# Linear attention with routed experts on one core: an earlier exponential table, a reordered key phase, and key features of five batches made by VectorE

## The reference, cut to what matters

```
xn   = layernorm(x)                        # per token, eps 1e-5
q, k = elu(xn @ Wq.T) + 1, elu(xn @ Wk.T) + 1     # 16 heads of 8
kv   = sum over the tokens of a batch of k^T v ; k_sum = sum of k
att  = (q kv) / (q k_sum + 1e-6) @ Wo.T
aff  = xn @ centroids.T ; e = argmax(aff) ; alpha = sigmoid(max aff)
h    = relu((layernorm(xn) * g[e] + b[e]) @ w1[e].T + b1[e])
out  = x + att + xn + alpha * (h @ w2[e].T + b2[e])
```

## Time and profile before

| | |
|---|---|
| median of 3 runs | 155.09 us |
| profiled execution | 155.4 us, span 153.6 us, granted clock 0.995 |
| PE busy | 138.0 us (90%) |
| DVE busy | 111.8 us (73%) |
| ACT busy | 101.4 us (66%) |
| POOL busy | 115.4 us (75%) |
| chain that ended last | PE 72%, POOL 9%, DVE 7%, ACT 5%, DMA 3% |

### The profile page before, as it was taken

The page is one execution under the profiler, slowest core; times in us unless marked ns, Lnnn a source line. Parts: engine busy times, 40 slices in busy tenths (PEclk is TensorE's granted clock), DMA queues, the critical chain, the costliest instruction groups (busy, mean ns, idle before and its releaser), DMA issues.

```text
span 153.6 us, 4729 instructions
## 1 busy us (share of the span) xinstructions
PE 138.0 (90%) x1138; PEld 131.5 (86%) x1138; DVE 111.8 (73%) x395; ACT 101.4 (66%) x334; POOL 115.4 (75%) x137
## 2 busy tenths in 40 slices
PE   3945999896999999999999999999999999999930
PEld 3945898796988998899999999999999999999920
DVE  3999998999968988897856554667777756556440
ACT  7533988999448786886666657666666666666610
POOL 7644430899958867888887768878888888877774
PEclk9999999999999999999999999999999999999997
DMA  4999200499937999677678998877777777841111
GB/s 142 327 323 420 94 4 0 151 344 294 274 89 214 241 340 286 163 201 192 161 195 233 287 338 205 216 190 207 196 166 174 189 160 174 135 41 53 51 51 51
DMA packets 26601, 29.10 MB, mean 189 GB/s; under 512 B 3024, under 2 KB 20432, under 8 KB 26448
## 3 DMA queue, kind: packets, MB, share of 16 engines
q1 hardware_dynamic: 21808, 23.69, 49.9%
q0 software_dynamic: 4480, 5.05, 17.8%
q10 hardware_dynamic: 288, 0.07, 0.2%
HBM read 18.18 MB, written 10.62 MB: 187 GB/s over the span
## 4 chain that ended last, share of the span: by engine, by line
PE 72%; POOL 9%; DVE 7%; ACT 5%; DMA 3%; issue 2%; SPq 1%; DVEq 0%
PE bank L718 22%; PE bank L706 21%; PE bank L671 6%; POOL out L417 5%; PE bank L688 5%; PE bank L659 4%; POOL feat_k L425 4%; PE bank L596 3%; DVE stats L770 3%; DMA x<-in_x 3%; PE bank L679 3%; PE bank L698 2%; PE bank L651 2%; DVE xn L818 2%; ACT k_exp L510 2%
## 5 line engine op out<-in xcount | busy, mean ns | idle before, releaser
L541 ACT ACTIVATE hT<-bank,b 128x128 f32<-128x128 f32 x156 | 44.6, 369 | 25.8 <-PE bank L706 25.7
L718 PE MATMUL bank<-w,hT 128*128 x312 | 42.8, 280 | 0.8 <-ACT hT L541 0.7
L706 PE MATMUL bank<-zT,feat_k 128*128 128x128 f32 x312 | 41.2, 275 | 0.0
L718 PEld LDWEIGHTS bank<-w,hT 128*128 128x128 f32 x312 | 37.8, 191 | 2.0 <-issue 1.2
L706 PEld LDWEIGHTS bank<-zT,feat_k 128*128 128x128 f32 x312 | 37.9, 192 | 0.0
L409 POOL DMA_INDIRECT out<-rows,token_at x20 | 32.0, 1602 | 6.1 <-issue 6.1
L396 POOL DMA_INDIRECT rows<-z_rows,token_at x20 | 20.6, 1030 | 5.0 <-issue 3.5
L1037 DVE TENSOR_SCALAR zT<-xn,ln_g,ln_b 128x128 f32 x39 | 14.2, 363 | 9.6 <-issue 8.7
L1052 DVE SCALAR_TENSOR_TENSOR rows<-y_own,weight,rows 128x128 f32 x39 | 13.8, 355 | 7.8 <-DVE y_own L1044 5.8
L425 POOL TENSOR_TENSOR feat_k<-feat_k,k_exp 128x256 f32<-128x256 f32 x16 | 14.2, 908 | 7.0 <-ACT k_exp L510 6.4
L396 POOL DMA_INDIRECT rows<-z_base_rows,token_at x12 | 12.0, 1000 | 4.0 <-issue 3.4
(11 more groups left out here) (124 smaller groups left out, 256.9 us busy)
## 6 DMA issues: line engine op xcount, KB each, us to landing
feat_k<-in_w1T SPq DMA_DIRECT2D x39, 256.0 KB, 4.1
z_rows<-xn SPq DMA_DIRECT2D x4, 528.0 KB, 5.0
z_base_rows<-xn SPq DMA_DIRECT2D x8, 264.0 KB, 5.4
x<-in_x SPq DMA_DIRECT2D x8, 256.0 KB, 4.8
w<-in_w2T SPq DMA_DIRECT2D x1, 2048.0 KB, 10.4
out<-x SPq DMA_DIRECT2D x8, 256.0 KB
z_base_rows<-x SPq DMA_DIRECT2D x16, 128.0 KB
b<-in_b SPq DMA_DIRECT2D x1, 512.0 KB, 5.8
```

The costliest lines, as they stand in the source:

```text
L541: last = a.activation(hT[:, par, c * P:(c + 1) * P], bank[hidden_bank(s)][:, c * P:(c + 1) * P], ACT.Relu, bias=b1[:, c, bass.ds(e, 1)])
L706: last = t_.matmul(bank[hidden_bank(s)][:, c * P:(c + 1) * P], w1_now[:, s % W1_RING * FC + c, :], zT[:, s % ZT_RING, :], start=True, stop ...
L718: last = t_.matmul(bank[y_bank(s)][:, 0:D], hT[:, par, c * P:(c + 1) * P], w2[:, bass.ds(e * (FC * D) + c * D, D)], start=(c == 0), stop=( ...
```

## The change

- In phase 1 the third square root and that of the second norm leave ScalarE. `rsqrts_of_both` makes rstd of chunk 2 (12 columns) and rstd_2 of all tiles (32 columns) on VectorE alone, from an integer guess and three Newton rounds over 44 columns. `second_norm` keeps two instructions.
- The exponential's table is loaded after copy_v(1), and exp_of_k(0) follows it there.
- `choose` works in three parts (tiles 0 to 15, 16 to 23, 24 to 31), in another order with the copies of values.
- For batches 7 to 11 (`SUM_BY_DVE`) ScalarE writes no max(k, 0) and GpSimd adds nothing: VectorE makes max(k, 0) + exp from the projection's bank (`features_k`), between `hot_lanes` and `mask_kv`. TensorE's project_k(11) to (15) wait for these, since they use the same banks again; so do the exponentials of 11 to 15, for the buffer.
- `ranks` moves behind keys_values(0), `tokens` behind keys_values(10).
- `staircase` and `words` move from ahead of `slot_tokens` into turns 1 and 2 of VectorE's attention loop. TensorE, ScalarE and VectorE wait for `expert_ready` only in turn 10.
- `EARLY` becomes 18 and `UNSCATTERED` 26.

```diff
-    CHOOSE = (0, 16, 32)
+    CHOOSE = (0, 16, 24, 32)
-    TOKENS_AT = 9
+    TOKENS_AT = 10
+    SUM_BY_DVE = (7, 8, 9, 10, 11)
-    EARLY = 20
-    UNSCATTERED = 27
+    EARLY = 18
+    UNSCATTERED = 26
...
             for b in range(NB):
+                if b in SUM_BY_DVE:
+                    continue
                 pool.wait_ge(k_exp_ready, b + 1)
...
+            a.activation(warm[:, :], mean[:, 0:1], ACT.Exp, scale=0.0)
+            exp_of_k(0)
             for gr in range(2, NG + LAG):
...
-                    if b == 2:
-                        sqrt_of(2)
-                        sqrt_of_second()
...
             def project_k(b):
                 if b >= K_EARLY + K_BANKS:
-                    pe.wait_ge(k_exp_ready, b - K_BANKS + 1)
+                    if b - K_BANKS in SUM_BY_DVE:
+                        summed(pe, b - K_BANKS)
+                    else:
+                        pe.wait_ge(k_exp_ready, b - K_BANKS + 1)
...
-            ranks()
             for b in range(TOKENS_AT + 1):
                 if b >= K_EARLY:
                     project_k(b + K_BANKS)
                 keys_values(b)
+                if b == 0:
+                    ranks()
...
+            def rsqrts_of_both(filling):
+                part = slice(CHUNK[NCH - 1], NT)
+                n = NT - CHUNK[NCH - 1]
+                dve.wait_ge(var_ready, NCH)
+                v_.tensor_scalar(raised[:, 0:n], var[:, part], EPS_LN, None, ALU.add)
+                step(v_.tensor_scalar(raised[:, n:n + NT], var[:, :], 1.0 + EPS_LN, EPS_LN * EPS_LN, ALU.mult, ALU.add), filling)
+                v_.tensor_scalar(halved[:, 0:n + NT], raised[:, 0:n + NT], -0.5, None, ALU.mult)
+                step(v_.tensor_scalar(guess[:, 0:n + NT].bitcast(i32), raised[:, 0:n + NT].bitcast(i32), -0.5, SEED, ALU.mult, ALU.add),
+                     filling)
+                for r in range(ROUNDS):
+                    step(v_.tensor_tensor(sq[:, 0:n + NT], guess[:, 0:n + NT], guess[:, 0:n + NT], ALU.mult), filling)
+                    step(v_.tensor_tensor(nw[:, 0:n + NT], sq[:, 0:n + NT], halved[:, 0:n + NT], ALU.mult), filling)
+                    if r < ROUNDS - 1:
+                        step(v_.scalar_tensor_tensor(guess[:, 0:n + NT], nw[:, 0:n + NT], 1.5, guess[:, 0:n + NT], ALU.add, ALU.mult),
+                             filling)
+                v_.scalar_tensor_tensor(rstd[:, part], nw[:, 0:n], 1.5, guess[:, 0:n], ALU.add, ALU.mult).then_inc(rstd_ready, 1)
+                step(v_.scalar_tensor_tensor(rstd_2[:, :], nw[:, n:n + NT], 1.5, guess[:, n:n + NT], ALU.add, ALU.mult), filling)
+                dve.wait_ge(rstd_ready, NCH)
...
+            def features_k(b):
+                dve.wait_ge(k_exp_ready, b + 1)
+                v_.scalar_tensor_tensor(feat_k[:, TB * b:TB * (b + 1), :].rearrange("p j d -> p (j d)"), k_bank(b)[:, 0:TB * P], 0.0,
+                                        k_exp[:, b % K_BANKS, :], ALU.max, ALU.add).then_inc(k_by_dve, 1)
...
             choose(0)
+            second_norm()
             copy_v(V_BY_DVE[0])
-            second_norm()
+            choose(1)
             for b in V_BY_DVE[1:]:
                 copy_v(b)
-            for c in range(1, len(CHOOSE) - 1):
-                choose(c)
+            choose(2)
...
+            features_k(7)
             hot_lanes(0)
+            features_k(8)
+            mask_kv(0)
             hot_lanes(1)
+            features_k(9)
             hot_lanes(2)
-            mask_kv(0)
+            features_k(10)
             hot_lanes(3)
+            features_k(11)
             mask_kv(1)
-            staircase()
+            slot_tokens()
             mask_kv(2)
-            words()
-            slot_tokens()
             mask_kv(3)
...
+                if j == 1:
+                    staircase()
+                if j == 2:
+                    words()
                 if j == WORDS_AT:
+                    dve.wait_ge(expert_ready, 1)
                     steps.word(0)
```

More of the change, by code:

```diff
@@ L226, in values_of, with summed @@
                 eng.wait_ge(v_copied, b + 1 - by_dve)
+        def summed(eng, b):
+            by_dve = [n <= b for n in SUM_BY_DVE].count(True)
+            if b in SUM_BY_DVE:
+                eng.wait_ge(k_by_dve, by_dve)
+            else:
+                eng.wait_ge(k_summed, b + 1 - by_dve)
         def hidden_bank(s):
@@ L484, in _, with exp_of_k @@
             expand_lanes(3)
+            def exp_of_k(b):
+                part, neg = b % K_BANKS, b % 2
+                act.wait_ge(k_done, b + 1)
+                if b >= K_BANKS:
+                    summed(act, b - K_BANKS)
+                a.activation(k_neg[:, neg, :], k_bank(b)[:, 0:TB * P], ACT.Relu, scale=-1.0).then_inc(k_neg_ready, 1)
+                if b not in SUM_BY_DVE:
+                    a.activation(feat_k[:, TB * b:TB * (b + 1), :].rearrange("p j d -> p (j d)"), k_bank(b)[:, 0:TB * P], ACT.Relu)
+                act.wait_ge(k_neg_ready, b + 1)
+                a.activation(k_exp[:, part, :], k_neg[:, neg, :], ACT.Exp, scale=-1.0).then_inc(k_exp_ready, 1)
             copy_xnT(0)
@@ L846, in _ @@
             moments(2, rows_1, rows_1)
[L847 to L850 removed]
+            rsqrts_of_both(rows_1)
             finish(rows_1)
```

51 lines of the change are left out of this document (15 added, 36 removed).

## The result

The changed kernel takes 158.63 us (median of four runs, 158.47 to 159.26) against 155.23 us for the kernel before in the same comparison: 1.0209 times as long, 95% interval 1.0148 to 1.0271. It is slower by 3.4 us, where 1.45 were forecast, and lies 0.6 us above the range of 154.0 to 158.0. The profiled execution takes 158.53 us, span 156.8 us, granted clock 0.984.

The account below looks back on a forecast made before the run. GpSimd's chain to the last scatter was taken to bound the end, TensorE having slack. Terms -0.5 + 1.2 + 0.75 = +1.45 us on the profiled 155.4 gave 156.85, so 156.5 for the median; eight in ten, 154.0 to 158.0.

Parts of the forecast that it names:

- The bound: Kernel's end: GpSimd's last uninterrupted stretch sets it, TensorE has slack; without GpSimd the span would end near 152.3, not 153.6.
- Normalising, +1.1: Normalising phase: ten dependent VectorE steps make rstd 1.23 us later, TensorE's next transposes 1.1 later; bounds 0.9 and 1.4.
- The table load: ScalarE's idle stretch of 2.50 us: load, small activation and exp_of_k(0) fit free, taking 1.3 to 1.5 us off its path.
- num(0), -0.5: Key phase: num(0) 0.5 us earlier, at 44.73, with VectorE's late scan as delay; bounds 2.4 earlier and 1.6 later.
- Staircase and words, +1.2: Attention loop: 1.98 us of moved VectorE steps, less slack of 0.70 and 0.1, delay the rest by 1.2; bounds 1.0 and 2.1.
- GpSimd's tail, +0.75: From base rows to the end: longer stretch +1.3, wait perhaps ending earlier -0.55, together 0.75 us later; bounds +0.1 and +1.3.
- The shorter GpSimd program: Rival at gather(18): if not held for base rows, GpSimd gains 2.9 us and the median is 154.5; chance 0.10.
- VectorE was not ahead: Rival in the key phase: VectorE ahead of TensorE, num(0) up to 2.4 us earlier, time 153.8 to 154.6; chance 0.18.
- The lock did stay: Rival in the key phase: sums and lanes in step at 1.21 us each, num(0) +1.6, at most 159.5; chance 0.10.

Follow-up runs that it names:

- e12: Changed kernel with GpSimd's sum of batch 0 held until the first choose has written its first maximum: 168.2 to 172.5 us on a chip with standstills, no ratio.
- e7: Changed kernel with no batch's features on VectorE, GpSimd adding all sixteen: 158.34 us, 1.0194 of the kernel before.
- e8: e3 with VectorE's features for batches 9 to 13 instead of 7 to 11: 155.80 us, 1.0045 of the kernel before.
- e3: Changed kernel with EARLY 20, UNSCATTERED 27, and staircase and words back ahead of slot_tokens: 0.9969 of the kernel before, on a chip with standstills.
- e5: Kernel before with only staircase and words moved into attention turns 1 and 2 and the expert_ready waits in turn 10: 156.43 us, 1.0117.
- e2: Changed kernel with staircase and words back ahead of slot_tokens, all else as changed: 1.0082 of the kernel before, on a chip with standstills.
- second execution: The same changed kernel run and traced once more, nothing altered: 158.95 us against 155.50 for the kernel before, 1.0251.
- e4: Kernel before with only EARLY 18 and UNSCATTERED 26: 1.0149 of the kernel before, on a chip with standstills.
- e9: Changed kernel with EARLY 20, UNSCATTERED 27, staircase and words ahead of slot_tokens, no features on VectorE: 156.03 us, 1.0074 of the kernel before.
- e10: e9 with two Newton rounds instead of three (factors less exact): 154.55 us, 0.9988 of the kernel before.
- e6: Changed kernel with two Newton rounds instead of three (factors less exact): 1.0228 of the kernel before; traced execution 160.38 us.
- e11: Changed kernel with EARLY 20 and UNSCATTERED 27, on a chip without standstills: 157.68 us, 1.0177 of the kernel before.

## Why the prediction was wrong, step by step

**The bound.** Right. The end belongs to GpSimd's last uninterrupted stretch, the saved gathers became a wait of 5.71 us ("some 4"), and TensorE's slack at the end grew: the last scatter starts 3.8 us behind the last accumulation, where it was 1.65.

**Normalising, +1.1.** rstd 3.22 behind var (3.16 forecast), later by 1.29. The rounds' worth is measured: 0.72 each, three steps of 0.24. The transposes started 4.58 behind var (20.06), against 4.37 forecast and 3.26 before. They waited 0.87 us for a tile of VectorE's, not for GpSimd's as I had written.

**The table load.** Right: 12.26 to 13.54, in the idle stretch, exponential of batch 0 at 14.19, and no late copy behind it. The small activation follows 0.01 us behind it (13.55), so again no drain of the kind that the Trainium skill names in "ScalarE: Activation LUTs", section "What ACT_TABLE_LOAD costs" (1.38 us), is to be seen. The forecast missed another thing: what an early table sets free on GpSimd.

**num(0), -0.5: the step that failed first, by 1.03 us.** Its sentence was "the scan at 28.9 instead of 27.97". That is 12.9 behind var; it came at 13.93, and everything behind kept nearly its forecast distance: scan to the tiles' one-hot 3.33 (3.38 forecast), one-hot 0.69 (0.68), the first feature at 34.07 with 33.55 forecast although var was 0.53 earlier, TensorE waiting for `feat_k` as said.

The rows behind var say where that microsecond went. The copy of batch 15 is done 11.21 behind var (26.69), forecast 10.59: 0.62 late. `choose(2)` takes 1.70 from there instead of 1.4: 0.30, of which 0.25 is its `rt_a` at 27.05, 0.52 beside a sum and 0.27 without one (24.91, the same form). The rest to the scan takes 1.02 instead of 0.9. The first part is the largest, and it fails a sentence of the normalising section: "Everything behind, to the last values at 25.6 instead of 24.5, is TensorE at its own pitch". The last values end at 25.87, which is 0.80 later behind var than forecast, and TensorE waits 0.32 for a copy of VectorE's on the way (24.70). VectorE was the late one: its first `choose` starts 3.41 behind rstd, 2.69 before the change. Of these 0.72 us, e12 shows 0.67 to come from GpSimd's early sum, by the normalising instruction of 0.88 us; and 0.31 of it reaches the scan.

Small instructions of 32 columns are held as well, a cast 0.71 us (28.31) and `pos_up` 0.75 (31.64), where 0.17 to 0.19 is the time without a sum. But that is no cause of the miss: `pos_up` stands behind the scan, and between the last `chosen` and the tiles' one-hot the kernel before loses about as much, 1.16 us (`alpha`, a 0.65 where 0.42 is usual, and `hi` with 0.59) against 1.11 for the two here. In its timeline:

```profile
26.98 0.69 DVE L897 TENSOR_SCALAR alpha<-alpha_e 128x32 f32<-128x32 f32 x1
...
37.66 1.22 POOL L425 TENSOR_TENSOR feat_k<-feat_k,k_exp 128x256 f32<-128x256 f32 x1
```

The prediction had priced this lock on the large lane operations only. It had their numbers right (0.69 without GpSimd, 0.89 and 1.21 with it), but from a row that it misread: the 0.68 of the earlier trace rows, at 37.61, is no row with an idle GpSimd. The sum at 37.66 stands beside it, starts 0.05 us behind it, and takes 1.22 instead of 0.73. There the sum was held, not VectorE. (The second one-hot took 1.10, not 1.02.) In the Trainium skill, "SBUF — State Buffer", section "Who interferes with whom", copy, cast and tensor_scalar can enter a mode that takes the port pair shared with GpSimd, and whoever is first blocks the other for its whole instruction. The trace agrees: the long ones named here are a tensor_scalar of 0.88, a cast of 0.71 and two tensor_scalar of 0.75 and 0.69. Each of them ends 0.04 to 0.08 us behind the end of a sum (22.19 behind 22.11, 29.02 behind 28.98, 32.39 behind 32.35, 27.67 behind 27.63), as an instruction does that could not run before. And `rt_a`, with two inputs, falls under the section's other sentence, the only one that I had used.

The remedy itself was weighed wrongly too. The prediction let VectorE's features replace GpSimd's sums, with the scan as the only delay; e7 shows that they cost 0.84 us net, with TensorE's project_k(11) and (13) waiting for them (0.81 and 0.38) in the changed kernel. e8, with later batches, has num(0) 0.62 earlier than e3, so it is the choice of batches.

**Staircase and words, +1.2.** Right, +1.25; e5, alone on the kernel before, +1.21, and e2, taken out, gives 24.65. The parts differ and nearly cancel: `past` took 0.44 us where I had 0.64, the reduction 0.44 for 0.35, the last cast 0.62 where e5 has 0.16; the two stretches take 2.06 us together, 1.98 forecast.

**GpSimd's tail, +0.75: the second step that failed, by 1.15.** It was the sum +1.3 less 0.55, from "so the wait may end 0 to 1.2 earlier". Three parts. The count of gathers and scatters gave +1.0, one gather ahead of the first scatter (1.25) less 0.26 in the scatters; that was sound, 0.3 under the forecast. The base rows were issued 0.25 later behind the experts' start, which was not foreseen. And the landing did not come earlier: I had taken some 2 us of way, which no row showed, and a gather held by its order. But the row of that gather in the earlier trace rows has 0.66 us of idle time ahead of it, where gathers held by their order alone have 0.17: it was waiting already before the change. The gather starts 4.10 us behind the start of the rows' issue here, 5.28 in the second execution, 4.33 before, and in none of the eighteen traces less than 4.10. Where it is 4.10, two later gathers wait 0.87 and 1.06 us, put down to earlier ones; where it is 5.28, they don't, and the sum is the same (16.67 and 16.65). What makes these stretches equal is open. From landing and waits together come +0.65 instead of -0.55. In the Trainium skill, "DMA: Bandwidth & Descriptors", section "Anatomy of one DMA — SWDGE (gpsimd) path", a fixed cost of about 2.0 us is named for a transfer, most of it the receipt from the target memory. That section is on GpSimd's path; these rows are of two stores that SyncE issues while experts' weights are fetched. From the end of their issue (1.01 us for both) to the gather it is 3.09 us here, so the figure falls short of what these stores took.

**The rivals.** The shorter GpSimd program did not count, since the gather is held (5.71 us of idle time, and 5.51 in e4). VectorE was not ahead. The lock did stay in part, though not where that rival put it, on the lanes (0.68 to 0.89, not 1.21): it held a normalising instruction and `choose`. The forecast's order of the terms was right, and 1.7 us were missing: 1.03 and 1.15 and 0.05 of them, less the 0.53 of an earlier start. What stays open: the early table, the root by Newton, the three parts of `choose` and the order of ranks and tokens never ran without each other. Together, with the rest undone, they are a loss or a tie (e9 at 1.0074, e10 with its less exact factors at 0.9988), so how much the early table gives back of the 1.29 us of the normalising is not shown.

## What to carry to other kernels

Work taken off an engine ahead of its wait for something else is no gain, and what is put behind that wait instead is paid in full: count the instructions between the last wait and the end, not all of them. A row with more idle time ahead of it than its neighbours (0.66 us among 0.17) is such a wait. When an early result sets an engine free to start sooner, list what will then run beside it, small instructions too: a sum of 0.7 us on GpSimd can hold a 0.17 us cast on VectorE for half a microsecond. Look for the same loss in the kernel before, though, ahead of calling it the cause. And a place where an engine waits is the right place for work that nobody needs yet; moved to where the engine is the one waited for, the same two microseconds cost 1.2.

## What the runs showed of the hardware

- VectorE's fp32 tensor_scalar over 128x128 takes 0.34 us and 0.88 us beside one GpSimd addition of 256 columns; with that addition held back the longest is 0.43 (e12).
- The lock goes both ways. In the kernel before, lane operations beside sums take 1.21 us, but the one at 37.61, which starts 0.05 us ahead of a sum, takes 0.68, and that sum takes 1.22 instead of 0.73. The start in the record does not always tell who is held: the normalising instruction of 0.88 us starts 0.06 ahead of the sum (21.32 and 21.38), while the one ahead of it on VectorE ran until 21.49.
- The granted clock fell to 0.50 for 2 us in e6 (0.93, 0.50 and 0.72 from 40 to 46 us) and ate 1.65 us: num(0) 0.93 later where 0.72 earlier was due. TensorE had been busy 7.45 of the 8 us from 34 to 42. In the other seventeen traces the clock stays at 1.00 from 40 to 46 us. Two rounds alone don't do it, since e10 has them too; what does is open.
- The kernel before took 155.1 to 155.5 us in three comparisons and 165.6 and 166.2 in the two on other chips. In the eight traces from the two, TensorE stands still for 8.2 to 12.3 us in the experts' phase (0.6 to 0.7 in the others), and in seven of them the granted clock from 90 to 100 us is 0.66 to 0.88 instead of 1.00. Why is open. Ratios taken there hid the tail's price.
- The 58.4 us from the first to the last scatter hardly depend on how the tiles are divided: two accumulating scatters fewer are two times 1.91 us, and against them stand two whole ones and a gather, at 1.27. Worked out that is a tie; measured it is 0.26 less from before to after, and 0.00 between e11 and the changed kernel.
